# A graph layer's row gather: one of 32 indirect gathers done as 128 one-row DMAs by byte offset, and all block transfers issued by ScalarE

## The chip, the cores and the metric

The kernel runs on one core of a Trainium2 chip. The metric is the device time of one execution in microseconds (us). Five engines run their own instruction streams side by side: TensorE (PE; its weight loads are shown as PEld), VectorE (DVE), ScalarE (ACT), GpSimd (POOL) and SyncE (SP). They wait for one another through semaphores only. A "q" behind an engine's name (SPq, DVEq) marks its sequencer: register work, branches, loads of registers and the issuing of DMAs. The core has 16 DMA engines, which carry the transfers that SP, ACT and POOL issue.

## The reference, cut to what matters

```python
def _gcn_layer(x, W, b, edge_weight, edge_src, edge_dst):
    support = x @ W
    msgs = support[edge_src] * edge_weight[:, None]
    agg = jax.ops.segment_sum(msgs, edge_dst, num_segments=N_NODES)
    return agg + b
# x: 12500 x 256 float32; 200000 edges, sorted by dst; dst = 12500 * u**2, src uniform
x = x + gnn(layernorm(x))      # two layers: elu(_gcn_layer(..., W1, b1)), elu(_gcn_layer(..., W2, b2))
x = x + ffn(layernorm(x))      # ffn: H = gelu(x @ W1 + b1), 256 -> 1024; softmax gate over 8 experts;
                               # the chosen expert's H @ Wd[e] + bd[e], times its probability
```

## The kernel before

**Stages.** From 0 to about 115 us the kernel normalises the rows of x into a table in HBM (`xn_scratch`), loads the edge lists and turns them into tables in SBUF. Then come two graph layers, of about 1,960 and 2,010 us. The second one also runs the dense part of the feed-forward on each block of 128 nodes as soon as the layer has finished it. From about 4,125 us on the nodes are sorted by expert and the experts' products run.

**A graph layer.** The edges are cut into 392 groups of 512, four tiles of 128 edges each. Eight groups are an iteration (`ITERS` = 49), four are a half. POOL (line 537) gathers for each tile 128 rows of 1 KB by indirect DMA: 32 gathers in an iteration, into a ring `rows` of 8 slots by 4 tiles. Before slot 0 and slot 4 it waits for `s_idx`, the indices that DVE stages (line 778) for half h+2 only after it has added the four groups of half h; before each slot it waits for `s_mm`, the products of the group that held the slot. DVE (line 847) builds for each group a matrix S of weights (128 edges by 96 nodes per tile). PE (line 1164) multiplies the rows by S, 8 products in a group; each ran as two MATMUL and two LDWEIGHTS. DVE (line 886) adds the result to `aggT` at the group's first node, and builds the S of the group after next (line 888). PE uses two buffers of S, so the third group after any point needs DVE's add of the first.

**Ticks.** After each half comes, by a table of numbers, a tick for one block of nodes (98 blocks, 98 halves). In layer 1 ACT copies the block out of `aggT` (line 625), PE multiplies it by the layer's weights (1174), DVE adds the bias (895), ACT and DVE form the elu, and SP stores the result to `h_scratch` (437). In layer 2 the tick also holds the feed-forward's steps for older blocks: PE lines 1186 to 1212, DVE 924 to 955, ACT 653 to 664, and on SP the load of x's block (452) and the stores of x1 (462) and of the hidden rows (467). DVE and ACT wait for those stores by `s_free` and `s_payfree`, which SP raises.

**Loops.** Each engine has its own hardware loop over the 49 iterations, with both halves written out. PE and DVE hold each half twice: with code for groups that reach past the 96 nodes of S, and without (lines 1237 and 973 choose). The loops turn at line 1233 (PE), 969 (DVE), 669 (ACT) and 529 (POOL); SP has one loop over the blocks in each layer (435, 473).

## Time and profile before

| | us |
|---|---|
| median of 3 runs | 4690.26 |
| lowest of the runs | 4685.44 |
| the profiled execution, its span | 4687.7 |
| POOL busy | 3267.9 (70%) |
| PE busy | 3478.1 (74%) |
| DVE busy | 1979.0 (42%) |
| ACT busy | 1116.6 (24%) |

The profile is of one execution. Its span runs from the first instruction to the last. Issuing a DMA, register work and branches are not counted as busy, so SP has no busy time, and POOL's busy time lacks the 0.3 us between two gathers. "Idle before it" in a row is the time that the engine stood still ahead of the instruction, with what ended it; "issue" there is time for which the profile shows no releaser.

### The profile page before, as it was taken

The page shows a single profiled execution, that of the slowest core. Times are in us where ns is not written, and L with a number is a line of the kernel's source. Part 1 is how long each engine was busy: PE and PEld are TensorE (multiplying, and loading weights), DVE is VectorE, ACT ScalarE, POOL GpSimd, SP SyncE. Part 2 cuts the span into 40 slices and gives each one's busy share as a digit, 9 for nine tenths or more (in the row PEclk, how much of TensorE's full clock was granted, in tenths as well). Part 3 has the DMA queues.
Part 4 walks back from the last instruction along what each step waited for, and adds up shares of the span by engine and source line. Part 5 has one row for each costly group of instructions (what it writes and reads, how often), then busy time and mean ns, then how long its engine had stood idle before and what let it go on. Part 6 is the DMA issues. An engine that isn't in the chain of part 4 may idle for free.

```text
span 4687.7 us, 84720 instructions
## 1 busy us (share of the span) xinstructions
PE 3478.1 (74%) x21458; PEld 3215.9 (69%) x21459; DVE 1979.0 (42%) x6592; ACT 1116.6 (24%) x1692; POOL 3267.9 (70%) x3405
## 2 busy tenths in 40 slices
PE   2766676676666666667877777777777777859999
PEld 1666666665666665657777777777777777748887
DVE  8333333333333333334454454445444444573333
ACT  4111111111111111113333333333333333311111
POOL 5777777777777777767777777777777777524444
PEclk7766666667666666669999999999999999889999
DMA  8333333333333333334444444444444444335554
GB/s 278 113 113 112 113 111 112 113 112 112 113 111 113 112 113 112 113 95 128 145 139 144 144 137 143 145 144 139 141 145 139 142 143 145 116 127 169 180 175 150
DMA packets 266657, 627.24 MB, mean 134 GB/s; under 512 B 63397, under 2 KB 135034, under 8 KB 265922
## 3 DMA queue, kind: packets, MB, share of 16 engines
q0 software_dynamic: 170688, 492.87, 36.6%
q1 hardware_dynamic: 95362, 129.30, 7.9%
q14 instruction: 595, 4.87, 0.3%
q8 instruction: 12, 0.20, 0.0%
HBM read 519.25 MB, written 103.63 MB: 133 GB/s over the span
## 4 chain that ended last, share of the span: by engine, by line
PE 40%; issue 21%; POOL 15%; DVE 11%; DVEq 5%; DMA 5%; ACT 2%; POOLq 0%; ACTq 0%; SPq 0%
PE pA L1164 23%; POOL rows L537 15%; PE pA L1286 8%; PE pB L1202 4%; DMA rows<-xn_scratch,idx 3%; DVE S L847 2%; PE pZ L1174 1%; ACT L653 1%; DVE work L929 1%; DVEq L359 1%; PE pC L1276 1%; PE pB L1276 1%; DVE work L924 1%; DVEq L876 1%; DVE aggT L886 1%
## 5 line engine op out<-in xcount | busy, mean ns | idle before, releaser
L1164 PE MATMUL pA<-S,rows 128*128 128x96 f32 x12544 | 2040.8, 337 | 716.0 <-DVE S L847 314.5
L1164 PEld LDWEIGHTS pA<-S,rows 128*128 128x128 f32 x12544 | 1966.6, 249 | 834.3 <-issue 421.7
L537 POOL DMA_INDIRECT rows<-h_scratch,idx x1568 | 1502.3, 958 | 516.5 <-issue 492.5
L537 POOL DMA_INDIRECT rows<-xn_scratch,idx x1568 | 1490.2, 950 | 485.2 <-issue 458.1
L886 DVE TENSOR_TENSOR aggT<-aggT,pA 128x192 f32 x784 | 277.3, 354 | 2061.0 <-PE pA L1164 1421.4
L625 ACT ACT_TABLE_LOAD x196 | 251.5, 1283 | 3002.5 <-DVE aggT L886 3000.4
L847 DVE TENSOR_SCALAR S<-iota_w,tdst,twgt 128x96 f32<-128x96 f32 x3152 | 843.9, 343 | 5.5 <-issue 2.6
L1174 PE MATMUL pZ<-wg,stage 128*128 128x256 f32 x784 | 295.2, 514 | 252.6 <-ACT stage L625 252.6
L1202 PE MATMUL pB<-work,w 128*128 128x128 f32 x3232 | 389.2, 279 | 33.2 <-DVE work L929 33.2
L1202 PEld LDWEIGHTS pB<-work,w 128*128 128x128 f32 x3232 | 370.1, 192 | 42.0 <-DVE work L929 42.0
L1286 PE MATMUL pA<-aggT,work 128*128 x1680 | 381.7, 380 | 0.0
L1174 PEld LDWEIGHTS pZ<-wg,stage 128*128 128x128 f32 x784 | 176.6, 250 | 296.8 <-ACT stage L625 275.6
L1286 PEld LDWEIGHTS pA<-aggT,work 128*128 128x128 f32 x1680 | 311.7, 191 | 39.5 <-issue 0.9
L562 POOL DMA_INDIRECT out_dram<-aggT,ids x105 | 107.2, 1021 | 226.6 <-DVE ids L1087 180.1
L1186 PE MATMUL pC<-identg,work 128*128 128x136 f32 x1236 | 164.5, 283 | 3.4 <-ACT work L664 1.8
L1105 DVE TENSOR_TENSOR aggT<-pA,aggT 128x256 f32<-128x256 f32 x105 | 44.6, 425 | 277.3 <-PE pA L1286 277.3
L1186 PEld LDWEIGHTS pC<-identg,work 128*128 128x128 f32 x1236 | 151.9, 192 | 4.0 <-issue 2.0
L557 POOL DMA_INDIRECT aggT<-pay_scratch,ids x105 | 101.6, 967 | 40.8 <-issue 34.0
L664 ACT ACT_TABLE_LOAD x100 | 128.3, 1283 | 1.8
L653 ACT ACT_TABLE_LOAD x100 | 128.3, 1283 | 1.7
L929 DVE TENSOR_TENSOR work<-pB,b1col 128x1024 f32<-128x1024 f32 x102 | 123.9, 1214 | 3.1 <-PE pB L1202 2.4
L901 DVE TENSOR_SCALAR zexp<-zexp 128x256 f32<-128x256 f32 x198 | 62.4, 315 | 134.2 <-ACT zexp L634 134.2
(175 smaller groups left out, 2107.9 us busy)
## 6 DMA issues: line engine op xcount, KB each, us to landing
pay_scratch<-work SPq DMA_DIRECT2D x98, 512.0 KB
rows<-xn_scratch,idx POOLq DMA_INDIRECT x1568, 2.8
rows<-h_scratch,idx POOLq DMA_INDIRECT x1568
h_scratch<-work SPq DMA_DIRECT2D x98, 128.0 KB
pay_scratch<-work SPq DMA_DIRECT2D x98, 128.0 KB, 2.5
work<-in_x_dram SPq DMA_DIRECT2D x97, 128.0 KB
rows<-in_x_dram SPq DMA_DIRECT2D x24, 512.0 KB, 5.2
xn_scratch<-rows SPq DMA_DIRECT2D x24, 512.0 KB, 5.9
```

Of the source, the lines that this page charges most:

```text
L537: pool.indirect_dma_start(rows[:, s, t, :], None, source, bass.IndirectOffsetOnAxis(at, 0))\
L625: act.activation(stage[:, :, :], aggT[:, :, block_of(j)], ACT.Copy).then_inc(s_stage[layer], 1)
L653: act.activation(bstd[:, 0:1], bmv[:, 1:2], ACT.Sqrt, bias=epsc[:, :]).then_inc(s_std2, 1)
L664: act.activation(HT, hid, ACT.Gelu).then_inc(s_gelu, 1)
L847: last = v.tensor_scalar(S[:, half, t, :], iota_w[:, :], tdst[:, t, bass.ds(g, 1)], twgt[:, t, bass.ds(g, 1)], ALU.is_equal, ALU.mult)
L886: v.tensor_tensor(to, to, pA[:, u % 2, 0:KC * W].rearrange("p (k n) -> p k n", k=KC), ALU.add)\
L929: v.tensor_tensor(hid, pB[:, :].rearrange("p (k n) -> p k n", k=KH), b1col[:, :].unsqueeze(2).to_broadcast([P, KH, P]), ALU.add).then_inc( ...
L1164: last = mm(to[:, k * W:(k + 1) * W], rows[:, slot, t, k * P:(k + 1) * P], Sx[:, t, :], start=(t == 0), stop=(t == T - 1))
L1174: last = mm(pZ[:, 0:C], stage[:, k, :], wg[:, k, :], start=(k == 0), stop=(k == KC - 1))
L1186: mm(pF[:, m // PERB, m % PERB, :], HT[:, m, :], identg[:, m, :], start=True, stop=True)
L1202: last = mm(pB[:, m * P:(m + 1) * P], w1[:, k, m * P:(m + 1) * P], xnT[:, k, :], start=(k == 0), stop=(k == KC - 1))
L1286: last = mm(pA[:, q % 2, 0:C], HTx[:, q % 2, m, :], wdk[:, m, bass.ds(ec, C)], start=(m == 0), stop=(m == KH - 1))
```

## The change

**Rows.** The last tile (t = 3) of the last slot (slot 7) in each iteration is no longer gathered by POOL. Its 128 rows come by 128 plain DMAs of one row each, 88 from SP and 40 from ACT, with the row's byte offset (index times 1024) in a register. POOL has 31 gathers in an iteration. The rows of even iterations go to `rows[:, 7, 3]`, those of odd ones to a new tile `xrow`. SP starts an iteration's batch once the first group of the iteration before is multiplied, ACT does its 40 in two lots of 20, ahead of the two ticks of the iteration before. Both wait, before a batch, for all their earlier rows.

**Offsets.** DVE shifts the last tile's indices to bytes; ACT stores them to HBM (`row_offsets`) in the first stage. SP and ACT load the next 88 and 40 offsets by a DMA of their own, and read them into registers with a TENSOR_LOAD of up to 32 registers each.

**Loops.** Because of the two buffers, PE, ACT and SP now loop over pairs of iterations (24 turns and one iteration written out behind them). DVE's and POOL's loops stay.

**Block transfers.** ACT issues all of them, at the end of its tick: the store to `h_scratch`, and in layer 2 the hidden rows, x1 and the next x block. SP's loops over blocks and `s_free`, `s_payfree` are gone; waits go to the stores' own semaphores. So that no block needs a special case, x is first copied, HBM to HBM, into `x_padded` (12.8 MB, by SP after the weights), and ACT waits for that copy before its first layer.

**Small.** `tsrc` is int16; `iota_w` and `tnum` are parts of `iota_p`.

```diff
+        def pairs(eng, body):
+            with eng.Fori(0, ITERS // 2) as q:
+                for par in range(2):
+                    body(2 * q + par, par)
+            body(ITERS - 1, (ITERS - 1) % 2)
...
+        def load_offsets(eng, layer, who, i):
+            n, lane = (XSP, XACT)[who], (0, XSP)[who]
+            row = i * -SLOTS + (XPAD + NG - SLOTS)
+            eng.dma_start(xoff[who][:, :], xoff_d[bass.ds(row, 1), lane:lane + n]).then_inc(s_ring[layer][who], 16)
+
+        def single_rows(eng, layer, who, i, par, first, last):
+            n, lane = (XSP, XACT)[who], (0, XSP)[who]
+            source = (xn_d, h1_d)[layer].rearrange("n c -> (n c)").bitcast(u8)
+            to = row_buffer(par).bitcast(u8)
+            for at in range(first, last, XREGS):
+                upto = min(at + XREGS, last)
+                if at == 0:
+                    hold(eng, s_mm[layer], SLOTS * i + 1)
+                    hold(eng, s_ring[layer][who], 16 * (i + 1))
+                _, values = nc.values_load_multi_w_load_instructions(
+                    xoff[who][0:1, at:upto], engines=[eng.engine], min_val=0, max_val=(N - 1) * ROWB,
+                    skip_runtime_bounds_check_because="a src is a node's number")
+                if at == 0:
+                    hold(eng, s_xrow[layer][who], 16 * (i * n + 1))
+                if upto == n:
+                    load_offsets(eng, layer, who, i + 1)
+                for k, v in enumerate(values, lane + at):
+                    eng.dma_start(to[k:k + 1, :], source[bass.ds(v, ROWB)].rearrange("(a n) -> a n", a=1))\
+                       .then_inc(s_xrow[layer][who], 16)
...
 SP
-            with sp.Fori(0, NB) as b:
-                sp.wait_ge(s_elu[0], b + 3)
-                sp.dma_start(h1_d[block_of(b), :], hout).then_inc(s_h1st, 16)
-                sp.wait_ge(s_h1st, 16 * (b + 1))
-                sp.sem_inc(s_free[0], 1)
...
+            sp.dma_start(xp_d[0:N, :], x[:, :]).then_inc(s_xpad, 16)
+            sp.dma_start(xp_d[N:NPAD, :], x[0:NPAD - N, :]).then_inc(s_xpad, 16)
+            sp.wait_ge(s_xoffst, 3 * 16)
+            for layer in range(2):
+                start_rows(sp, layer, 0)
+                pairs(sp, lambda i, par: single_rows(sp, layer, 0, i, par, 0, XSP))
+                sp.wait_ge(s_ring[layer][0], 16 * (ITERS + 1))
...
 POOL
-                        for t in range(T):
+                        for t in range(XT if s == SLOTS - 1 else T):
...
 ACT, layer 1's tick and layer 2's
+                act.wait_ge(s_elu[0], j + 2)
+                act.dma_start(h1_d[block_of(j - 1), :], hout).then_inc(s_h1st, 16)
...
-                act.wait_ge(s_payfree, j + 1)
+                act.wait_ge(s_payst, 16 * (j + 1))
...
+                act.wait_ge(s_payc, j + 2)
+                act.dma_start(pay_d[block_of(j - DEPTH), 0:HID], payh).then_inc(s_payst, 16)
+                if flows(1, j):
+                    act.wait_ge(s_elu[1], j + 2)
+                    act.dma_start(pay_d[block_of(j - 1), HID:PAY], x1).then_inc(s_x1st, 16)
+                if flows(0, j):
+                    act.dma_start(xb, xp_d[block_of(j), :]).then_inc(s_xb, 16)
...
+            def iteration(layer, i, par):
+                for half in range(2):
+                    if not isinstance(i, int):
+                        single_rows(act, layer, 1, i + 1, 1 - par, half * XACT // 2, (half + 1) * XACT // 2)
+                    h = 2 * i + half
+                    _, start, end = half_flags(act, h)
+                    ticks(act, start, end, lambda j: (tick1, tick2)[layer](j, h))
+
+            act.wait_ge(s_xoffst, 3 * 16)
+            act.wait_ge(s_xpad, 2 * 16)
             for layer in range(2):
+                start_rows(act, layer, 1)
+                single_rows(act, layer, 1, 0, 0, 0, XACT)
+                pairs(act, lambda i, par: iteration(layer, i, par))
...
 PE
             for layer in range(2):
-                with pe.Fori(0, ITERS) as i:
-                    for half in range(2):
...
+                pairs(pe, lambda i, par: iteration(layer, i, par))
```

**SP, the loop of layer 1.** Before, one turn of the loop stores one block; the rows are the whole loop (a DMA's row names where it writes and what it reads).

```order
L435 UNCONDITIONAL_BRANCH
L435 ISA
L437 ISA
L437 DMA h_scratch<-work 128x256
L438 ISA
L435 REGISTER_ALU
L435 COMPARE_AND_BRANCH
```

Now one iteration's part of the loop reads as follows (`xoff_sp` holds the 88 offsets); the loop holds it twice, the second time with `xrow` for `rows`.

```order
L334 ISA
L420 TENSOR_LOAD xoff_sp
L334 ISA
L428 DMA rows<-xn_scratch 1x1024 x32
L420 TENSOR_LOAD xoff_sp
L428 DMA rows<-xn_scratch 1x1024 x32
L420 TENSOR_LOAD xoff_sp
L408 ISA
L408 DMA xoff_sp<-row_offsets 1x88
L428 DMA rows<-xn_scratch 1x1024 x24
```

SP went from one store per tick to 89 DMAs and three loads of registers per iteration.

**ACT, between two ticks of layer 2.** Before, the GELU of one tick (L664) is followed by the loop's own rows and the next half's flags (L359).

```order
L664 ACT_TABLE_LOAD
L664 ACTIVATE work<-work 128x1024
L370 REGISTER_ALU
L370 COMPARE_AND_BRANCH
L369 UNCONDITIONAL_BRANCH
L359 ISA
L359 TENSOR_LOAD regs
```

Now, from the tick's last transfer (L699) to the next half's flags (L370):

```order
L699 DMA work<-x_padded 128x256
L381 REGISTER_ALU
L381 COMPARE_AND_BRANCH
L380 UNCONDITIONAL_BRANCH
L420 TENSOR_LOAD xoff_act
L408 ISA
L408 DMA xoff_act<-row_offsets 1x40
L428 DMA xrow<-h_scratch 1x1024 x20
L370 ISA
L370 TENSOR_LOAD regs
```

Three transfers at the tick's end and 20 rows with their register load now stand between one tick of ACT and the next.

## Rows read from the trace of the kernel before

**Rows 1.** The page's first line.
```profile
span 4687.7 us, 84720 instructions
```
**Rows 2.** Windows of equal stages: window, length, PE, PEld, DVE, ACT, POOL busy (count), clock, DMA share, GB/s.
```profile
0.00:120.00 120.00, 28.66 (x140) 25.17 (x141) 95.87 (x342) 48.85 (x89) 60.97 (x69) 0.72 0.88 274
230.00:1200.00 970.00, 667.51 (x3282) 604.89 (x3281) 312.85 (x1157) 130.91 (x240) 734.76 (x773) 0.65 0.39 112
2260.00:3200.00 940.00, 737.24 (x5507) 701.47 (x5506) 462.52 (x1564) 336.29 (x460) 705.82 (x737) 0.92 0.48 142
```
**Rows 3.** Line 537, all instructions: duration ns min/median/max, first and last start.
```profile
L537 POOL DMA_INDIRECT rows<-xn_scratch,idx x1568: 942/946/1256, 89.9 to 2056.4; - x196
```
**Rows 4.** Timeline of layer 1, POOL and PE: start, busy, [idle before, releaser].
```profile
1007.04 0.95 POOL L537 DMA_INDIRECT rows<-xn_scratch,idx  x1 [0.30 <-issue]
...
1011.27 3.70 PE L1164 MATMUL pA<-S,rows 128*128 128x96 f32 x16 [0.90 <-DMA rows<-xn_scratch,idx]
```
**Rows 5.** Waits in layer 1, window 100:2040: total us, times, longest.
```profile
PE pA L1164 <- DMA rows<-xn_scratch,idx: 227.3, 124, 3.1
```
**Rows 6.** Waits in layer 2, window 2260:4070: total us, times, longest.
```profile
PE pA L1164 <- DVE S L847: 169.7, 45, 4.3
POOL rows L537 <- DVE idx L778: 23.1, 37, 1.0
```
**Rows 7.** Timeline of PE over one iteration of layer 2, from tick to tick.
```profile
3018.79 7.51 PE L1164 MATMUL pA<-S,rows 128*128 128x96 f32 x64 [1.04 <-issue]
...
3034.34 0.38 PE L1212 MATMUL pT<-ident,work 128*128 128x128 f32 x2
3036.29 3.78 PE L1164 MATMUL pA<-S,rows 128*128 128x96 f32 x32 [1.57 <-issue]
3043.84 6.55 PE L1164 MATMUL pA<-S,rows 128*128 128x96 f32 x32 [3.76 <-DVE S L847]
...
3059.71 0.54 PE L1164 MATMUL pA<-S,rows 128*128 128x96 f32 x3 [0.90 <-issue]
```
**Rows 8.** Sequencers at the loops' turns in that iteration (lines 969, 876, 1233; start last).
```profile
L969 DVEq COMPARE_BRANCH  x1: 72/72/72, 3034.2 to 3034.2; - x1
L969 DVEq FUSED_REGOPS  x1: 93/93/93, 3037.6 to 3037.6; - x1
L973 DVEq COMPARE_BRANCH  x1: 72/72/72, 3038.7 to 3038.7; - x1
L876 DVEq FUSED_REGOPS  x3: 71/190/190, 3041.3 to 3045.0; - x3
L1233 PEldq FUSED_REGOPS  x1: 74/74/74, 3034.7 to 3034.7; - x1
```
**Rows 9.** SP's queue: one-row DMAs and their neighbours, and a DMA with its address in a register.
```profile
3.15 0.23 SPq L394 DMA_DIRECT2D aggT<-in_dst_dram  x1
3.42 0.40 SPq L390 DMA_DIRECT2D aggT<-in_src_dram  x1
L437 SPq MOVE h_scratch<-work x98: 29/29/29, 144.2 to 2071.6; - x98
```
**Rows 10.** Line 359, a load of one register on ACT's sequencer, and SP's store landing.
```profile
L359 ACTq TENSOR_LOAD <-regs x196: 264/268/462, 113.5 to 4056.4; - x196
DMA to landing us min/median/max: 1.7/2.5/3.2
```
**Rows 11.** Timeline of ACT in layer 2, first and last of a tick and the next.
```profile
3010.15 1.28 ACT L625 ACT_TABLE_LOAD   x1 [16.77 <-DVE aggT L886]
...
3016.50 1.06 ACT L664 ACTIVATE work<-work 128x1024 f32<-128x1024 f32 x1
3027.13 1.28 ACT L625 ACT_TABLE_LOAD   x1 [9.57 <-DVE aggT L886]
```
**Rows 12.** Timeline around the start of layer 1: SP's last load, ACT's first tick.
```profile
92.47 0.53 SPq L429 DMA_DIRECT2D b1col<-in_L_ffn_b_dram  x1
126.69 1.28 ACT L625 ACT_TABLE_LOAD   x1 [33.97 <-DVE aggT L886]
```

More of the change, by code:

```diff
@@ L85, in bass_gnn_then_routed_ffn @@
     KWIN = (N - 1) // W
+    XT = T - 1
+    XSP, XACT, XREGS = 88, 40, 32
+    XPAD = 2 * SLOTS
+    ROWB = 4 * C
     LNC = NB // T
@@ L269, in bass_gnn_then_routed_ffn @@
         s_elu = [sem(f"elu_ready_{l}") for l in range(2)]
-        s_free = [sem(f"elu_store_done_{l}") for l in range(2)]
         s_eln = [sem(f"elu_step_{l}") for l in range(2)]
@@ L372, in ticks, with source_stored, row_buffer, start_rows @@
                                             "the table's last end is the number of blocks"))
+        def pairs(eng, body):
[3 more added lines that the diff above has]
+            body(ITERS - 1, (ITERS - 1) % 2)
+        def source_stored(eng, layer):
+            if layer == 0:
+                eng.wait_ge(s_xst[0], 16 * (LNI + 2))
+                for s in range(1, SLOTS):
+                    eng.wait_ge(s_xst[s], 16 * LNI)
+            else:
+                eng.wait_ge(s_h1st, 16 * (NB + 2))
+        def row_buffer(par):
+            return xrow[:, :] if par else rows[:, SLOTS - 1, XT, :]
+        def load_offsets(eng, layer, who, i):
[21 more added lines that the diff above has]
+                       .then_inc(s_xrow[layer][who], 16)
+        def start_rows(eng, layer, who):
+            eng.sem_inc(s_xrow[layer][who], 16)
+            load_offsets(eng, layer, who, 0)
+            source_stored(eng, layer)
         @block.sync
@@ L521, in _ @@
             for layer, source in ((0, xn_d), (1, h1_d)):
-                if layer == 0:
-                    pool.wait_ge(s_xst[0], 16 * (LNI + 2))
-                    for s in range(1, SLOTS):
-                        pool.wait_ge(s_xst[s], 16 * LNI)
-                else:
-                    pool.wait_ge(s_h1st, 16 * NB)
+                source_stored(pool, layer)
                 with pool.Fori(0, ITERS) as i:
@@ L1158, in _, with products @@
             pe.sem_inc(s_y, 2)
-            def products(slot, Sx, to, semaphore):
+            def products(slot, par, Sx, to, semaphore):
                 for k in range(KC):
                     for t in range(T):
-                        last = mm(to[:, k * W:(k + 1) * W], rows[:, slot, t, k * P:(k + 1) * P], Sx[:, t, :],
+                        edge = row_buffer(par) if slot == SLOTS - 1 and t == XT else rows[:, slot, t, :]
+                        last = mm(to[:, k * W:(k + 1) * W], edge[:, k * P:(k + 1) * P], Sx[:, t, :],
                                   start=(t == 0), stop=(t == T - 1))
@@ L1225, in edges_half, with iteration @@
                                 pe.wait_ge(s_ovS[layer], w + 1)
-                                products(s, Sov, pOV, s_ovmm[layer])
+                                products(s, par, Sov, pOV, s_ovmm[layer])
                     pe.wait_ge(s_S[layer], g + 1)
                     pe.wait_ge(s_add[layer], g + 1)
-                    products(s, S[:, s % 2, :, :], pA[:, s % 2, :], s_mm[layer])
+                    products(s, par, S[:, s % 2, :, :], pA[:, s % 2, :], s_mm[layer])
             pe.wait_ge(s_w, 8 * 16)
-            for layer in range(2):
-                with pe.Fori(0, ITERS) as i:
-                    for half in range(2):
-                        h = 2 * i + half
-                        ovf, start, end = half_flags(pe, h)
-                        with pe.If(ovf > 0):
-                            edges_half(layer, i, h, half, True)
-                        with pe.Else():
-                            edges_half(layer, i, h, half, False)
-                        ticks(pe, start, end, (tick1, tick2)[layer])
+            def iteration(layer, i, par):
+                for half in range(2):
+                    h = 2 * i + half
+                    ovf, start, end = half_flags(pe, h)
+                    with pe.If(ovf > 0):
+                        edges_half(layer, i, par, h, half, True)
+                    with pe.Else():
+                        edges_half(layer, i, par, h, half, False)
+                    ticks(pe, start, end, (tick1, tick2)[layer])
+            for layer in range(2):
+                pairs(pe, lambda i, par: iteration(layer, i, par))
             for j in range(NB, NB + DEPTH):
```

102 lines of the change are left out of this document (48 added, 54 removed).

## The prediction

> **What bounds the kernel now.** I read the windows of equal stages first. In layer 1 POOL issues 773 gathers in 970 us, one in 1.255 us; in layer 2 it issues 737 in 940 us, one in 1.275 us [rows 2]. A gather is 0.95 us of work and 0.30 us of gap [rows 3, 4]. So an iteration of 32 gathers takes 40.2 us in layer 1 and 40.8 in layer 2, and at first sight POOL bounds both layers.
>
> The waits tell the layers apart. In layer 1 PE waits for the gathered rows, 124 times for 227 us [rows 4, 5]. There POOL is the bound. In layer 2 no wait of PE's products for gathered rows stands in the list: what they wait for is S from DVE, and it is POOL that waits, for the indices that DVE stages after finishing a half, 37 times, up to 1.0 us each [rows 6]. The timeline of one iteration says what PE does instead. It runs slots 4 to 7 at once (7.51 us), a tick until 3034.72, slots 0 and 1 from 3036.29, stands 3.76 us, slots 2 and 3 until 3050.39, the next tick, and is back at slot 4 at 3059.71 [rows 7]. From 3018.79 to 3059.71 is 40.9 us, the same 40.8 as above, and none of it is a wait for gathers. So PE's chain sets layer 2's period, and POOL, ready some 8 groups ahead, only fills it.
>
> The 3.76 us come from DVE. At its loop's turn the branch is at 3034.2 and the next instruction at 3037.6, 3.3 us later; the branch that skips the overflow code is at 3038.7, the next instruction at 3041.3, 2.5 us later. PE turns its loop in the same place within 0.2 us [rows 8]. I read this as DVE fetching code that a jump left behind, and PE finding its own at hand.
>
> **The sum.** It is made against this execution's span of 4687.7 us [rows 1]; the median of the runs, 4690.26, is 2.6 us above it, and is used as span plus 2.6.
>
> Layer 1, one gather less. 49 x 1.25 us = **-61 us**, if nothing else becomes the bound. SP must deliver its 88 rows within 31 x 1.25 = 38.8 us. The nearest row is the one-row load of line 394: 0.23 us of issue, and 0.27 us from start to the next start; with its address in a register a DMA has a MOVE of 0.03 us ahead of it, about 0.07 us with its gap [rows 9]. I take 0.355 us a row, between 0.34 and 0.37: 88 rows are 31.2 us. The offsets' own DMA is 0.45 us, the holds some 0.35 us, and the wait for the earlier rows to land, after the last issue, about 2 (a store lands in 1.7 to 3.2 us [rows 10]), under which the first register load can hide. That is 34 us plus two register loads. A load of one register takes 0.27 us [rows 10]; a load of 32 is not in the trace. Its bounds are 0.27 us and 32 x 0.27 = 8.6 us. It is one instruction, so I take 0.3 to 1.5 us, near the lower end: SP needs 35 to 37 us and is in time. The point from which it is not is (38.8 - 34) / 2 = 2.4 us a load. ACT's 40 rows are 14.2 us in a period in which it works some 7 in layer 1: hidden.
>
> The start of layer 1. ACT now waits for the 12.8 MB copy, which SP issues behind its last load at 93.0 [rows 12]. The first stage moved 274 GB/s with the DMA engines 88% busy [rows 2], so the copy takes at least 12.8 MB / 311 GB/s = 41 us, and at most 95 if gathers take their 112 GB/s beside it and reads and writes of HBM hinder each other. I take 47 (the 274): the copy ends at 140. Then ACT loads offsets (2.5), issues 40 and 20 rows (21.3) and comes to its first tick at about 165; before it did so at 126.69 [rows 12]. POOL starts at 89.9 [rows 3] and can run to the end of half 2, 12 groups or 59 us, so to 149; for half 3 it needs DVE through half 1, which is ACT's tick (5 us) and four groups (9 us) later: 179. **+30 us**, with 24 to 78 as bounds.
>
> Layer 2, one gather less: **0**. PE's chain does not wait for POOL; POOL's shorter iteration turns into longer waits for indices.
>
> Layer 2, PE's longer loop. The loop now holds two iterations. From the order of instructions, with each product as four (front: 8 products are 16 MATMUL and 16 LDWEIGHTS), PE's body in layer 2 grows from about 1,170 instructions to about 2,350, in layer 1 from 950 to 1,900. The trace shows a body of some 500 on DVE that stalls at each turn and one of 1,170 on PE that does not. Whether 2,350 does is open: below, nothing; above, DVE's 3.3 us at each turn and 2.5 us at each of four jumps over overflow code [rows 8], 13.3 us a turn. I think the turn and the first jump miss (5.8 us), and that 3.75 of it hides behind the wait for DVE at the same place [rows 7], leaving 2.1; for the three later jumps I take a third of 2.6, 0.9 each, since DVE's own code has mostly arrived by its second jump. 4.8 us x 24 turns = **+115 us**, bounds 0 and 230. In layer 1 PE has waits for gathers to use up, and I cost it at nothing.
>
> The Trainium skill (Runtime: NRT & Kernel Launch, Instruction fetch mechanics) says that PE's instruction memory holds 2,048 instructions and the other engines' 512, and that a taken branch outside the window waits for a fetch. By it layer 2's body is too long and layer 1's just fits, which is the term above; the trace agrees as far as its two bodies go.
>
> ACT in layer 2. In the shorter gap it starts ticks at 3010.15 and 3027.13, 17.0 us apart, and works until 3017.56 [rows 11]. It now adds three transfers (1.35 us), the offsets' DMA (0.45), 20 rows (7.1), a register load (0.3 to 1.5) and flags (0.9): 7.4 + 10.1 + 0.3 to 1.5 = 17.8 to 19.0. It is late by 0.8 to 2 us in one tick of two, but PE's own stalls stretch the same gap. I take 0.2 us x 49 = **+10**, bounds 0 and 100. DVE's waits on the stores are the old ones; the x block is asked for some 3 us later than before and has half a period to land.
>
> The tail: SP no longer sits behind the last stores and loads the experts' weights some 25 us earlier, into the last ticks' stores: **+2**. The small edits: 0, DVE's extra work lies in the first stage beside the x loads.
>
> Sum: -61 + 30 + 0 + 115 + 10 + 2 = +96; 4687.7 + 96 + 2.6 = 4786 us.
>
> **The rivals.**
> *No stall on PE.* The longer body finds its code as now. For it: PE shows no gap at any turn [rows 8]. Then -61 + 30 + 10 + 2 = -19: about 4670.
>
> *SP becomes the bound.* If a load of 32 registers takes 4.3 us (half of the upper bound), SP needs 34 + 9 + 2 = 45 us per iteration in both layers: +5 x 49 + 4 x 49 over today, +30: about 5160, and 5,700 at the upper bound. It decides from 2.4 us a load. For it: the one-register load is almost all round trip. Against: one instruction, one address. The Trainium skill (same page and section) gives some 200 ns per register even in bulk; by that a load of 32 would be 6.4 us, SP would need about 50 us, and the time be near 5,500. No run yet shows it.
>
> *Every jump misses.* 230 us instead of 115: about 4900.
>
> *Both layers shorten.* If in layer 2 it is POOL after all that paces PE, through the indices, then 2 x 61 less, with a start-up of 30: about 4600. Against it: PE's waits have no gathers in layer 2 [rows 6].
>
> **How the numbers follow.** Forecast 0.38 (own range 4730 to 4850); no stall 0.22; SP the bound 0.18; every jump 0.12; both shorten 0.10. The predicted time is the first's, 4786. The range leaves out the last and most of SP's: 4640 to 5150. Faster by over 2% (below 4596, about what this measurement can tell from no change) needs both layers: 0.08. Within 2% (to 4784) are the no-stall case, half of the forecast's own spread, and the rest of the last: 0.42. Slower 0.50.
>
> **What would show it.** Gathers per us on POOL: one in 1.25 with 31 an iteration in layer 1, 38.8 us; 40.8 or more in layer 2, with longer waits for indices. A gap on PE's sequencer between the loop's branch and the next instruction, 2 to 3.5 us, in layer 2 only. SP's register loads: their duration decides the third case at once. ACT's first tick of layer 1 near 165. I am wrong about layer 2 if its iterations get shorter than 40.8, and about SP if its rows stand back to back with PE waiting for them in slot 7.

## The result and the profile after

The changed kernel takes 5097.44 us (median of 4 runs, 5094.62 to 5102.15), against 4687.85 us before: a ratio of 1.0876, 95% interval 1.0859 to 1.0894. The forecast was 4786. Some of the experiments' kernels first ran while the kernel before itself took 6591 to 6918 us; their times are not compared with those of the table below, and all but one of them ran again beside a kernel before of some 4685 us (labels with b or c).

The windows and the gathers' line show where the 407 us between the two spans lie. First the page's first line, then windows as in [rows 2] with the start of layer 1 ahead of them, and that start in the kernel before; then POOL's gathers as in [rows 3] (line 555 is the old 537).

```profile
span 5094.6 us, 111092 instructions
```
```profile
90.00:230.00 140.00, 43.89 (x224) 39.95 (x225) 44.74 (x119) 15.78 (x21) 67.77 (x72) 0.57 0.58 178
230.00:1200.00 970.00, 595.76 (x3445) 542.55 (x3445) 333.30 (x1213) 136.37 (x250) 733.61 (x770) 0.70 0.41 118
2260.00:3200.00 940.00, 661.00 (x4560) 630.57 (x4560) 378.83 (x1291) 277.00 (x381) 561.88 (x588) 0.84 0.40 120
```
```profile
90.00:230.00 140.00, 84.55 (x456) 77.62 (x456) 65.25 (x201) 21.81 (x36) 106.28 (x111) 0.67 0.44 119
```
```profile
L555 POOL DMA_INDIRECT rows<-xn_scratch,idx x1519: 940/946/1204, 91.8 to 2050.6; - x190
L555 POOL DMA_INDIRECT rows<-h_scratch,idx x1519: 940/946/1191, 2068.1 to 4465.7; - x190
```

Layer 1: 770 gathers in 970 us against 773, so 31 take 39.05 us and 32 took 40.16. That is 54 us in 49 iterations, but layer 2 starts only 7.7 us earlier (2068.1, before 2075.8): the start of layer 1 gave back 46. Layer 2: 588 gathers in 940 us, 49.6 us an iteration against 40.8; from first to last gather 2397.6 us against 1999.4, **+398**. Behind the last gather the kernel runs for another 628.9 us against 612.5, +16. Together -8 + 398 + 16 = +406.

What PE does in layer 2, as in [rows 7], from two windows of its timeline:

```profile
3031.07 10.32 PE L1218 MATMUL pA<-S,rows 128*128 128x96 f32 x64 [5.19 <-issue]
...
3050.27 0.41 PE L1266 MATMUL pT<-ident,work 128*128 128x128 f32 x2 [0.68 <-ACT work L687]
3054.15 8.21 PE L1218 MATMUL pA<-S,rows 128*128 128x96 f32 x54 [3.47 <-issue]
...
3073.13 0.38 PE L1266 MATMUL pT<-ident,work 128*128 128x128 f32 x2
3080.42 9.58 PE L1218 MATMUL pA<-S,rows 128*128 128x96 f32 x64 [6.91 <-issue]
```

Two things are new. PE stands 5.2 and 6.9 us ahead of halves, with no releaser. And 3.5 us are lost ahead of a half in which nothing of PE's is slow (3054.15). A half has 32 products, each two MATMULs with a weight load ahead of each: 64 parts. The 64 parts behind a long stand take 9.6 to 10.3 us. That alone is not new: in [rows 7] one half of an iteration took 7.51 us, and the other 3.78 + 6.55 = 10.3 around the 3.76 us for which PE waited for S. The long stands are explained by PE's own branches. A turn of the doubled loop has four halves: here the third begins at 3031.07, the fourth at 3054.15 (10 of its parts stand in rows of their own), the next turn's first at 3080.42. The first three rows are the turn (line 388), the branch over the overflow code (1296) in the first half behind it, and the same in the third half; the fourth row has all turns between 2200 and 4450 us. Below them is the old loop's turn, over both layers.

```profile
L388 PEldq COMPARE_BRANCH  x1: 5247/5247/5247, 3071.4 to 3071.4; - x1
L1296 PEldq COMPARE_BRANCH  x1: 2344/2344/2344, 3077.6 to 3077.6; - x1
L1296 PEldq COMPARE_BRANCH  x1: 4173/4173/4173, 3026.5 to 3026.5; - x1
L388 PEldq COMPARE_BRANCH  x22: 4397/4827/5367, 2281.4 to 4353.8; - x22
```
```profile
L1233 PEldq COMPARE_BRANCH  x98: 73/216/223, 145.9 to 4095.5; - x98
```

On PE the stall is the branch's own duration; on DVE it was a gap behind a short branch [rows 8]. With the other two branches over overflow code (0.36 and 0.44) it is some 12 us in two iterations. The page's list of DMA queues shows the same as traffic, first after, then before. Queue q8 is the one that carries PE's code: e1 below, which changes nothing but PE's loops, has 489 packets on it and q14 as before.

```profile
q8 instruction: 489, 8.01, 0.7%
q14 instruction: 956, 7.83, 0.5%
```
```profile
q14 instruction: 595, 4.87, 0.3%
q8 instruction: 12, 0.20, 0.0%
```

8.01 MB in 489 packets is 16.4 KB each, about ten at each of 48 turns; before, PE's queue carried 12 packets in all. The Trainium skill (Runtime: NRT & Kernel Launch, Instruction fetch mechanics) has code come in blocks of 16 KiB, 256 instructions; the packets' size agrees.

### The profile page after: what moved, and what is told of

Same layout as the page of the kernel before. It is cut to its first block, busy times and chain, and to the rows that moved or that the text cites. A ratio compares the mean times of both kernels' runs of the same rounds, so it can differ in the third digit from the quotient of the medians.

```text
span 5094.6 us, 111092 instructions
## 1 busy us (share of the span) xinstructions
PE 3427.8 (67%) x21458; PEld 3181.0 (62%) x21459; DVE 1980.3 (39%) x6594; ACT 1116.8 (22%) x1692; POOL 3172.0 (62%) x3305
## 3 DMA queue, kind: packets, MB, share of 16 engines
q8 instruction: 489, 8.01, 0.7%
## 4 chain that ended last, share of the span: by engine, by line
PE 38%; issue 28%; ACTq 17%; DVE 8%; ACT 3%; DMA 3%; DVEq 2%; POOL 1%; SPq 0%; POOLq 0%
PE pA L1218 22%; ACTq L428 12%; PE pA L1348 7%; PE pZ L1228 4%; PE pB L1256 4%; ACTq L420 3%; ACTq L370 1%; DVE S L900 1%; ACT stage L651 1%; DVE work L982 1%; DMA x_padded<-in_x_dram 1%; PE pC L1338 1%; PE pB L1338 1%; ACT L681 1%; DMA pay_scratch<-work 1%
## 5 line engine op out<-in xcount | busy, mean ns | idle before, releaser
L1218 PE MATMUL pA<-S,rows 128*128 128x96 f32 x12352 | 1952.1, 334 | 964.8 <-issue 867.2
L1218 PEld LDWEIGHTS pA<-S,rows 128*128 128x128 f32 x12352 | 1908.9, 248 | 1060.6 <-issue 998.5
L555 POOL DMA_INDIRECT rows<-h_scratch,idx x1519 | 1450.7, 955 | 964.4 <-DVE idx L830 510.1
L555 POOL DMA_INDIRECT rows<-xn_scratch,idx x1519 | 1446.3, 952 | 521.2 <-issue 455.1
L900 DVE TENSOR_SCALAR S<-iota_p,tdst,twgt 128x96 f32<-128x96 f32 x3152 | 836.9, 340 | 10.1 <-issue 10.1
```

Of the source, the lines that this page charges most:

```text
L555: pool.indirect_dma_start(rows[:, s, t, :], None, source, bass.IndirectOffsetOnAxis(at, 0))\
L900: last = v.tensor_scalar(S[:, half, t, :], iota_w[:, :], tdst[:, t, bass.ds(g, 1)], twgt[:, t, bass.ds(g, 1)], ALU.is_equal, ALU.mult)
L1218: last = mm(to[:, k * W:(k + 1) * W], edge[:, k * P:(k + 1) * P], Sx[:, t, :], start=(t == 0), stop=(t == T - 1))
```

## Experiments

For each kernel: layer 1 and layer 2 from first to last gather, the time behind the last gather, the median, and the ratio to the kernel before that ran beside it. The bodies of PE's loop are given as counts of instructions; these are estimates from the order of instructions, as in the prediction.

| kernel | layer 1 | layer 2 | behind | median us | ratio (95%) |
|---|---|---|---|---|---|
| before | 1966.5 | 1999.4 | 612.5 | 4688 | |
| after | 1958.8 | 2397.6 | 628.9 | 5097 | 1.088 (1.086 to 1.089) |
| e1, PE's pairs alone | 1969.3 | 2076.2 | 611.5 | 4766 | 1.017 (1.015 to 1.019) |
| e10b, the same, code shifted | 1973.2 | 2151.9 | 614.9 | 4840 | 1.033 (1.032 to 1.035) |
| e2, after, PE's loop short | 1959.1 | 2006.6 | 620.0 | 4697 | 1.002 (1.001 to 1.003) |
| e3, after, ACT without rows | 1945.3 | 2201.3 | 625.5 | 4882 | 1.042 (1.040 to 1.044) |
| e4, both | 1943.0 | 1999.7 | 626.7 | 4678 | 0.998 (0.997 to 0.999) |
| e5b, after, ACT's hold earlier | 1959.0 | 2221.6 | 625.9 | 4918 | 1.049 (1.047 to 1.051) |
| e6b, after, copy waited later | 1951.7 | 2393.7 | 630.0 | 5083 | 1.084 (1.083 to 1.086) |
| e8b, rows in layer 1 only | 1949.4 | 2005.0 | 623.1 | 4690 | 1.001 (1.000 to 1.002) |
| e9, that without the copy | 1924.0 | 1998.0 | 611.5 | 4651 | 0.993 (0.991 to 0.994) |
| p1c, before, 385 dead instructions | 1969.7 | 2552.6 | 625.5 | 5259 | 1.123 (1.121 to 1.125) |

**PE's code against ACT's rows (e1 to e4).** The theory of PE's code: its long branches make layer 2. The rival: ACT's rows do, and the branches lie in PE's waiting time. e1 is the kernel before with

```diff
-                with pe.Fori(0, ITERS) as i:
+                with pe.Fori(0, ITERS // 2) as q:
+                    for par in range(2):
+                        iteration(layer, 2 * q + par)
+                iteration(layer, ITERS - 1)
```

> The kernel before, and only PE's loops turn every two iterations (24 turns and one iteration written out); gathers, SP, ACT, DVE stay. Theory 1, PE's code: in the changed kernel PE's branch at the loop's turn takes up to 5.2 us in layer 2 and the branches over the overflow code 2.3 and 4.2 us, about 12 us in two iterations, and the products behind them run at the lower clock. Then the same branches take as long here, layer 2's iteration grows from 40.8 to 46 to 48 us, layer 1 stays at 40.2 (POOL paces it), and the time is 4940 to 5030. Theory 2, ACT: the 400 us of layer 2 come from ACT's rows, which hold up its ticks, and PE's long branches lie in time in which PE would wait for ACT anyway. Then this kernel is within 30 us of before, 4690 to 4720.

e2 is the changed kernel with

```diff
-                        edge = row_buffer(par) if slot == SLOTS - 1 and t == XT else rows[:, slot, t, :]
+                        edge = rows[:, slot, XT - 1, :] if slot == SLOTS - 1 and t == XT else rows[:, slot, t, :]
...
-                pairs(pe, lambda i, par: iteration(layer, i, par))
+                with pe.Fori(0, ITERS) as i:
+                    iteration(layer, i, 0)
```

> The changed kernel, but PE's loops turn every iteration, with one iteration's code, as before. So that this needs no second buffer in the code, PE's product for the last tile of slot 7 reads the tile beside it (rows[:, 7, 2]) and not the single rows; the single rows are still fetched and waited for. The output is not the reference's. Theory 1, PE's code: the long branches are gone, layer 2's iteration falls from 49.4 to 43 us or less (ACT's lateness of some 3 us in one half stays), time 4720 to 4800. Theory 2, ACT: layer 2 stays at 47 us or more, time above 4980.

So e2 multiplies tile 2 of slot 7 in place of tile 3, and its output is not the reference's. e3 drops ACT's `single_rows`, their offsets and PE's wait for them (88 of 128 rows are fetched, so its output is not the reference's either); e4 has both edits.

> The changed kernel without ACT's 40 rows and their offsets in either layer (128 fetched rows become 88; xrow is cleared once by POOL; the output is not the reference's). ACT still issues all block transfers. Theory 1, PE's code: the long branches stay, and only what ACT's lateness costs goes: layer 2's iteration 46 to 48 us, time 4930 to 5030. Theory 2, ACT: layer 2's iteration back to 41 us, time 4680 to 4710.

> Both edits together: PE's one-iteration loops (last tile of slot 7 read from rows[:, 7, 2]) and no rows from ACT; output not the reference's. Both theories: layer 2's iteration is back at 40.8 us or a little under, layer 1 stays at 39.2 us, and the time is 4650 to 4690. If it is above 4720, a third cause is at work (SP's row transfers beside the gathers, or ACT's block transfers).

Measured: 4766, 4697, 4882 and 4678. e1 lies between the theories, e2 better than the first one had it, e3 below it, e4 as expected. The four corners show how much belongs to each part and how much only to both together:

| layer 2, us | ACT without rows | ACT with rows |
|---|---|---|
| PE's loop short | 1999.7 | 2006.6 |
| PE's loop long | 2201.3 | 2397.6 |

PE's code costs 202 us without ACT's rows; ACT's rows cost 7 us without PE's long code; another 189 come only where both are. SP's rows and ACT's block transfers are both in e4 and cost layer 2 nothing. Two questions followed: why PE's code costs 77 alone and 202 in this company, and how ACT's rows come to cost 196.

**The place of the code (e10b).** e1 with 14 instructions more ahead of layer 2's loop, 6 that run and 8 that never do:

```diff
+                if layer == 1:
+                    _, never, _ = half_flags(pe, 0)
+                    with pe.If(never > 200):
+                        for _ in range(2):
+                            mm(pOV[:, 0:W], rows[:, 0, 0, 0:P], Sov[:, 0, :], start=True, stop=True)
```

> As e1 (the kernel before, PE's loops in pairs), with 14 more instructions of PE's ahead of layer 2's loop, 8 of them never run: the loop's code stands 14 instructions later, where it stands in the changed kernel. PE's edit cost 77 us alone (e1) and 204 beside the single rows and ACT's transfers (e3 against e4). Theory 1, the place of the code decides where PE runs out of it: a pause of 2 to 3 us moves into a group, once in two iterations, with the lower clock behind it, layer 2 grows by 60 to 120 us, time 4825 to 4885. Theory 2, the other transfers (SP's rows, ACT's stores) take PE's slack away or make the fetch slower: as e1, 4760 to 4775.

Measured 4840: the first theory. PE's timeline where the pause stands, e1, then e10b:

```profile
3056.61 2.00 PE L1164 MATMUL pA<-S,rows 128*128 128x96 f32 x16 [1.09 <-issue]
3060.18 5.60 PE L1164 MATMUL pA<-S,rows 128*128 128x96 f32 x48 [1.57 <-DVE aggT L886]
```
```profile
3009.22 1.21 PE L1164 MATMUL pA<-S,rows 128*128 128x96 f32 x9 [1.09 <-issue]
3012.19 8.05 PE L1164 MATMUL pA<-S,rows 128*128 128x96 f32 x55 [1.76 <-issue]
```

A part is two instructions, a weight load and a matmul. 14 instructions of shift moved the pause from behind the 16th part to behind the 9th: 7 parts, 14 instructions. It stands there in all 22 pairs of iterations that were read in each trace (behind the 10th part in e3, behind the 7th in e5b and the changed kernel). So PE pauses at a fixed place of the code, which I read as running out of it; the releaser named in e1's row is by the way. In e1 the 48 parts behind it take 5.60 us at a granted clock of 1.00; in e10b the 55 behind it take 8.05 at 0.79. The changed kernel:

```profile
3004.95 1.78 PE L1218 MATMUL pA<-S,rows 128*128 128x96 f32 x7 [3.53 <-issue]
...
3008.80 8.67 PE L1218 MATMUL pA<-S,rows 128*128 128x96 f32 x57 [2.08 <-issue]
```

Over all of layer 2 it reads as follows. Each number is the stand ahead of a half plus its 64 parts, pauses and waits for S included, in us: the mean of the 22 pairs. The doubled loop turns ahead of half 1; the kernel before turns ahead of halves 1 and 3.

| | half 1 | half 2 | half 3 | half 4 | clock in half 2 |
|---|---|---|---|---|---|
| before | 15.5 | 8.5 | 15.6 | 8.5 | 1.00 |
| e1 | 18.2 | 10.1 | 13.6 | 8.5 | 0.99 |
| e10b | 18.1 | 13.1 | 14.4 | 8.5 | 0.77 |
| e3 | 18.0 | 13.9 | 15.0 | 9.4 | 0.73 |
| e5b (below) | 18.5 | 14.3 | 15.4 | 9.6 | 0.75 |
| after | 18.1 | 16.2 | 15.5 | 13.1 | 0.66 |

e1 and e10b differ by 3.0 us in half 2, the one with the pause, where the clock falls, and by 0.8 in half 3. These make the 76 us between their layers 2, of the 125 that separate e1's from e3's. The other 49 are spread over halves 2 to 4 and were not separated: they come with the other parts of the change.

**ACT's hold (e5b).** In the changed kernel ACT stands after its tick until PE has multiplied the first group of the next iteration. Its rows are not late because they are long, but because they begin late:

```profile
3024.71 0.69 ACTq L699 DMA_DIRECT2D work<-x_padded  x1
...
3035.00 0.35 DVE L939 TENSOR_TENSOR aggT<-aggT,pA 128x192 f32 x1 [9.92 <-PE pA L1218]
...
3036.57 7.00 ACTq L428 DMA_DIRECT2D rows<-h_scratch  x20
...
3041.59 0.36 DVE L939 TENSOR_TENSOR aggT<-aggT,pA 128x192 f32 x1 [0.46 <-PE pA L1218]
```
```profile
3045.08 1.28 ACT L651 ACT_TABLE_LOAD   x1 [19.36 <-DMA rows<-h_scratch]
```

From 3025.7 to 3034.8 ACT does nothing; PE's group ends at 3034.8, ACT loads registers and issues 20 rows, and comes to its tick at 3045.08, 3.1 us after the half's last add (3041.59 + 0.36). In layer 2's waits that is a row that e3 and e5b don't have (window 2260:4400):

```profile
DVE zexp L954 <- ACT zexp L660: 116.1, 42, 4.0
```

DVE's tick is late by almost as much, and PE's next half waits for the tick's last result. Most of the 3.47 us ahead of 3054.15 is that; with the earlier hold (e5b) 1.53 are left at the same place. The edit:

```diff
-                    hold(eng, s_mm[layer], SLOTS * i + 1)
+                    hold(eng, s_mm[layer], SLOTS * i + (1 if who == 0 or isinstance(i, int) else 0))
```

> The changed kernel with one number changed: inside the loops ACT starts its rows when the iteration's last group before has been multiplied, and not one group later (the tile that the rows go to is free by then). Output is the reference's. Theory 1, the hold: ACT's 20 rows cost 215 us (5097 against 4882) because PE, late from its long branch, releases them only with its first group, and ACT then comes to its tick some 3 us after the half is added. With the earlier release ACT issues them while PE stands: 4885 to 4930. Theory 2, the length of ACT's work (20 rows, register load, offsets and turn, some 11 us in each half) is what costs: 5040 or more.

Measured 4918: the first theory. 176 of the 196 us go with one count of one semaphore. By the table above 1.9 us go in half 2 and 3.5 in half 4, where the clock rises from 0.77 to 0.97; the rest lies in the ticks. ACT's rows of the same place now begin while PE stands in its long branch (3048.3 to 3054.0), and the tick follows the add:

```profile
3050.06 7.06 ACTq L428 DMA_DIRECT2D rows<-h_scratch  x20
3065.10 1.28 ACT L651 ACT_TABLE_LOAD   x1 [16.95 <-DVE aggT L939]
```

**How long PE's loop may be (p0b, p1c).** The kernel before, with products behind a condition that is never true at the end of layer 2's loop: 12 groups' worth (385 instructions), or 6 (190).

```diff
+                        with pe.If(start > 200):
+                            for _ in range(12):
+                                products(0, Sov, pOV, s_ovmm[1])
```

> The kernel before with some 385 instructions never run at the end of PE's loop in layer 2 (body about 1,560 in place of 1,170). In p1b, against a kernel before of 6905 us, the loop's turn took 5.8 us, the branch over the padding 3.8 and every second branch over the overflow code some 3.7. Theory 1: such branches cost time as in e1, where 256 us of them in layer 2 made 77: with some 500 us of them here, 4850 or more. Theory 2, nearly all of it hides in PE's waits: 4690 to 4740.

> The kernel before with some 190 instructions never run at the end of PE's loop in layer 2: a body of about 1,365 instead of 1,170. In p0 (ratio 1.000, against a kernel before of 6905 us) no branch of the loop was longer than 0.3 us. Theory 1, the body still fits: branches of 0.22 us, time 4680 to 4700. Theory 2, the length of the body costs something by itself, in proportion: half of what p1c showed, 4900 or more.

p1c measured 5259, +576 us, for code that never runs: the first theory. Its turn (line 1233), the branch over the dead code (1243), and below them the turn in p0, the first run of p0b's kernel:

```profile
L1233 PEldq COMPARE_BRANCH  x45: 4617/5112/6152, 2246.2 to 4564.7; - x45
L1243 PEldq COMPARE_BRANCH  x45: 3739/4494/5044, 2241.8 to 4560.0; - x45
```
```profile
L1233 PEldq COMPARE_BRANCH  x98: 73/216/237, 177.0 to 6313.5; - x98
```

With a body of about 1,365 instructions no branch of layer 2's iterations is longer than 0.5 us, in p0 and in p0b (ratios 1.000 and 0.9985; the kernel before took 6905 and 6918 us beside them, so the forecast times could not be tested and no price is read from them, only the branches). With about 1,560 every turn is slow. For this loop the limit lies between. It is not a matter of doubling the loop.

**The start of layer 1 (e6b, e8b, e9).** e6b moves ACT's wait for the copy to layer 2.

> The changed kernel, but ACT waits for the copy of x into x_padded only before layer 2, where it first reads it. Output is the reference's. Theory 1: the wait for the copy is what delays layer 1's first tick (from 126.7 to about 180 us) and costs 30 to 40 us: 5057 to 5067. Theory 2, the copy's traffic beside the gathers and ACT's 60 rows cost it (as in e8b, where 33 gathers fewer were issued by 230 us although nobody waited for the copy): 5085 or more.

Measured 5083, -14 us: two us short of the second theory's bound, and 16 above the first one's range. The first tick moved from 179.8 to 164.5, and layer 1 gained 7 us by it. e8b has single rows in layer 1 alone; it also has e5b's hold and e6b's later wait.

> Single rows in layer 1 only; in layer 2 POOL gathers all 32, and PE and ACT loop over single iterations; the copy is waited for before layer 2; ACT's hold is the earlier one; ACT issues all block transfers. Output is the reference's. Theory 1: layer 1 keeps its gain of 1 us in an iteration (39.2 against 40.2) and layer 2 is as before: 4640 to 4665. Theory 2: block transfers on ACT or the copy cost something of their own in the unchanged layer 2: 4690 or more.

Measured 4690, at the second theory's bound and 25 us above the first one's range; but layer 2 is only 6 us longer than before, and its own trace shows the rest at the start. PE waits 21 us for a group's gathers, in just the time in which the copy runs (50.3 us from issue to landing; 48.6 in the changed kernel):

```profile
93.33 3.23 SPq L494 DMA_DIRECT2D x_padded<-in_x_dram  x1
...
140.51 3.70 PE L1221 MATMUL pA<-S,rows 128*128 128x96 f32 x16 [21.08 <-DMA rows<-xn_scratch,idx]
```

From 90 to 230 us POOL issues 78 gathers, 72 in the changed kernel, and 111 in the kernel before (both in the section on the result). e9 takes the copy away: in layer 2 SP does the block transfers as before.

> As e8b (single rows in layer 1 only, 4689 us there), and without the copy of x: in layer 2 SP loads x's blocks and stores the hidden rows and x1 as in the kernel before, ACT issues only layer 1's stores. Output is the reference's. In e8b PE waited 21 us for the second group's gathers while the copy ran, POOL issued 78 gathers from 90 to 230 us where the kernel before issued 111, and layer 2 and the tail took 6 and 10 us more than before. Theory 1, the copy's traffic holds up the start: layer 1 runs at 38.9 us an iteration from the start, about 1915 to 1930 us, the rest is as before: 4630 to 4655. Theory 2, ACT's 60 rows ahead of the first tick and the rows themselves cost the start: 4665 to 4690.

```profile
90.00:230.00 140.00, 64.21 (x349) 57.81 (x350) 57.17 (x167) 20.34 (x31) 93.43 (x97) 0.62 0.41 113
```
```profile
L588 POOL DMA_INDIRECT rows<-xn_scratch,idx x1519: 940/946/1471, 91.5 to 2015.5; - x190
```

Measured 4651, the first theory; ratio 0.993 (0.991 to 0.994): of the versions with the reference's output the only one that beats the kernel before, by less than 1%. 97 gathers by 230 us, layer 1 42.5 us shorter. At the kernel before's pace 1519 gathers take 1906 us; against that the changed kernel loses 53, e6b 46, e8b 43 and e9 18. So the wait for the copy is worth some 7 us, the copy's own traffic 25 to 28, and 18 are left. As much later e9's first tick comes (144.9 against 126.69), ACT's first 60 rows standing ahead of it.

**The first runs of these kernels.** Their expectations, mostly in the words of the repeats':

> The changed kernel with one number changed: inside the loops ACT starts its rows when the iteration's last group before has been multiplied, and not one group later (the tile that the rows go to is free by then). Output is the reference's. Theory 1, the hold: ACT's 20 rows cost 215 us (5097 against 4882) because PE, late from its long branch, releases them only with its first group, and ACT then comes to its tick some 3 us after the half is added. With the earlier release ACT issues them while PE stands: 4885 to 4930. Theory 2, the length of ACT's work (20 rows, register load, offsets and turn, some 11 us in each half) is what costs: 5040 or more.

> The changed kernel, but ACT waits for the copy of x into x_padded only before layer 2, where it first reads it. Output is the reference's. Theory 1: the wait for the copy is what delays layer 1's first tick (from 126.7 to about 180 us) and costs 30 to 40 us: 5057 to 5067, first tick near 150 (ACT's own 60 rows still stand ahead of it). Theory 2: the copy's traffic beside the gathers and ACT's rows cost it: 5085 or more.

> Single rows in layer 1 only; in layer 2 POOL gathers all 32 and PE and ACT loop over single iterations; the copy is waited for before layer 2; ACT's hold is the earlier one; ACT issues all block transfers. Output is the reference's. Theory 1: layer 1 keeps its gain of 1 us in an iteration (39.2 against 40.2) and layer 2 is as before: 4640 to 4665. Theory 2: block transfers on ACT or the copy cost something of their own in the unchanged layer 2: 4690 or more.

> The kernel before, with some 390 instructions of code that is never run (12 groups' products behind a condition that is never true) at the end of PE's loop in layer 2: the body grows from about 1,170 to 1,560 instructions, of which 1,170 run. If the body's length decides from about 1,900 on, no branch of PE's is longer than 0.5 us and the time is 4680 to 4700. If it decides earlier, the loop's turn takes 3 to 5 us; most of it lies in the 3.8 us for which PE waits for S there, and the time is 4690 to 4740.

> As e1 (the kernel before, PE's loops in pairs), with 14 more instructions of PE's ahead of layer 2's loop, 8 of them never run: the loop's code stands 14 instructions later, where it stands in the changed kernel. PE's edit cost 77 us alone (e1) and 204 beside the single rows and ACT's transfers (e3 against e4). In the traces the one difference inside PE's products is a pause in the middle of a group, once in two iterations (24 in layer 2, 2.3 us each, in e3 and the changed kernel, with the lower clock behind it; in e1 PE stands 1.6 us between two groups and keeps its clock). Theory 1, the place of the code decides where PE runs out of it: the pause moves into a group here too, layer 2 grows by 60 to 120 us, time 4825 to 4885. Theory 2, the other transfers (SP's rows, ACT's stores) make the fetch slower or take PE's slack away: as e1, 4760 to 4775.

> As p1: the kernel before with some 385 instructions never run at the end of PE's loop in layer 2 (body about 1,560 in place of 1,170). In p1, against a kernel before of 6591 us, the loop's turn took 5.9 us and the branch over the padding 3.7 us. The same branches are as long here; about 3.8 us of each turn hide in the wait for S. Theory 1: 9 to 11 us of branches a turn, 4 to 7 of them on the path, in 49 turns: 4880 to 5030. Theory 2, nearly all of it hides: 4690 to 4740.

> The same with some 190 instructions never run: body about 1,365. If the limit lies between 1,365 and 1,560, no branch of PE's in layer 2 is longer than 0.5 us, and the time is 4685 to 4700. If 1,365 is already past it, the turn takes 3 to 6 us.

e5 took 7186 us, e6 7116 and e8 7233 beside a kernel before of 6591 (ratios 1.089, 1.080, 1.098), p1 6763 in its one run; e10 6937, p1b 7035 and p0 6903 beside 6905 (1.006, 1.019, 1.000), p0b 6905 beside 6918. The same edits rank otherwise there than in the table, so those times decide nothing here. What is used from them is how long PE's branches are: 5.8 us at p1's and p1b's turn, 0.22 at p0's and p0b's (medians).

## Why the prediction was wrong, step by step

**Layer 1, one gather less:** -61 forecast, -54 measured; no run explains the 7 between. SP was in time, by little: its rows come every 0.345 us (32 in 11.05), but a load of 32 registers takes 2.04 us where I took 0.3 to 1.5, and the case turned at 2.4. (The rival's upper bound was added up wrongly: two loads of 8.6 us give SP 53 us and a time near 5,960, not 5,700.)

```profile
L420 SPq TENSOR_LOAD <-xoff_sp x294: 1673/2038/3297, 142.0 to 4441.6; - x147
```
```profile
PE pA L1218 <- DMA xrow<-xn_scratch: 2.3, 1, 2.3
```

The second row is all that PE waited for single rows between 300 and 2000 us. 2.04 us for 32 registers is 64 ns each; the rule of some 200 ns per register (Trainium skill, Runtime: NRT & Kernel Launch, Instruction fetch mechanics) does not hold here.

**The start:** +30 forecast, +46 measured. The copy ended about where I had it (94.7 + 48.6 = 143, forecast 140), the first tick came at 179.8 and not at 165. The step that failed is that POOL "can run to the end of half 2". It stopped one half earlier, at 130.7, because PE had no rows to multiply while the copy ran, and so finished half 0 at 153.5 and not at 125.9:

```profile
136.41 3.70 PE L1218 MATMUL pA<-S,rows 128*128 128x96 f32 x16 [15.20 <-DMA rows<-xn_scratch,idx]
146.83 6.72 PE L1218 MATMUL pA<-S,rows 128*128 128x96 f32 x32 [6.72 <-DMA rows<-xn_scratch,idx]
```

I priced the wait for the copy and not its traffic, which is three to four times as much. That the sum came within 16 us is luck: the wait, which made all of my 30, is worth 7.

**Layer 2, one gather less:** 0, right. e4, with all that remains, has 1999.7 us against 1999.4.

**PE's longer loop:** +115 forecast. The mechanism was right: slow branches in the long body, in layer 1 hidden (e1's layer 1 is 2.8 us longer, though the same loop's turn takes some 3.7 us in the changed kernel's), in layer 2 not. Alone it is 77 (e1), below my term, since more of it hides than the 3.75 us that I took: the wait for S goes in both iterations of a pair, and half 3 is even shorter than before. e1's waits of layer 2 have 11 us left of the 170 for S [rows 6]. With the code near its place in the changed kernel it is 152 (e10b, whose pause is two parts from the changed kernel's), beside the other parts 202 (e3 less e4). What the term lacked is a pause in the middle of straight code, whose place 14 instructions decide, and the lower clock behind it: half 2 takes 13.1 us in place of 8.5. The parts behind the turn are no slower than before; there PE had lost its clock behind the wait for S already. Branch for branch I had 5.8 us for the turn and the first jump and 0.9 for each later one, 8.5 in all; measured are 7.6 for the first two, 4.2 for the third half's and 0.4 for the others, 12 in all.

**ACT in layer 2:** +10 forecast, +196 measured beside PE's long loop; this is the step that failed most: 186 of the 311 us by which the forecast was short. The length of ACT's work was right (with the loop short it costs 7; that its terms add to 9.8 and not to 10.1 changes nothing), and the sentence that "PE's own stalls stretch the same gap" was wrong. By the change ACT waits until the first group is multiplied (the `hold` on `s_mm`), and I never asked what that wait does when PE is the one that is late: PE's stall doesn't make room for ACT's rows, it moves their release. From the release to the half's last add PE and DVE need 6.8 us (3034.8 to 3041.6); ACT needs 10.3 to its tick.

**The tail:** +2 forecast, +16 measured. 4 of the 16 are layer 2's own slowness: from the last gather to the end of the last block's multiplication by the layer's weights it takes 24.6 us against 20.6 (31.5 in p1c, where nothing of the tail was changed). Behind that point it is 604.3 against 591.9, +12. Here the mechanism was named (the experts' weights come earlier, into the last stores), its size was not: the 8 MB are asked for at 4484.80, 35 us earlier against that multiplication and not 25, and ACT then waits for its hidden-row stores,

```profile
4484.80 22.88 SPq L504 DMA_DIRECT2D aggT<-in_L_ffn_Wd_dram  x8
```
```profile
ACT work L685 <- DMA pay_scratch<-work: 14.8, 4, 7.6
```

where the kernel before had no such wait. In e9, with the old order of SP's loads and stores, the tail is back at 611.5. That the weights and not the stores' new place on ACT lengthen those waits was not tested.

**The whole:** 4687.7 - 8 + 398 + 16 = 5094. Of layer 2's 398, 152 are PE's longer code near its place, 176 ACT's hold, 20 the rest of ACT's rows, and 49 are PE's code beside the other parts, left open. Against the forecast 186 us are missing in ACT's term, 87 in PE's (202 for 115), 16 at the start, 14 in the tail and 7 in layer 1's gather. The hold's 176 and the rest's 20 exist only beside PE's long code. The measured time lies inside the outer range of 4640 to 5150, but that range reached so high for SP as the bound, which did not come; that it holds is luck. Of the rivals, "no stall on PE", SP as the bound and the shorter layer 2 fell; "every jump misses" was nearest for PE (230 for 202), and none of them had ACT in it.

## What to carry to other kernels

Before a loop is unrolled for a second buffer, count the body, with the code in it that is jumped over: past a limit (here between some 1,365 and 1,560 instructions on PE) every turn pays, and dead code counts like live code. When an engine gets work behind a wait, ask who raises the semaphore, and what happens when that engine is late; a wait set one count too strict cost more here (176 us) than the long loop near its place (152), though only beside it. A copy with nobody waiting for it is still paid by the transfers beside it, so do without it (e9), or try to put it where the DMA engines are idle (not tried here).

## What the runs showed of the hardware

- PE's slow branch: 4.4 to 5.4 us at the turn of a body of about 2,350 instructions, 4.6 to 6.2 with about 1,560, 0.22 (median) with about 1,170 and 1,365. By the Trainium skill (Runtime: NRT & Kernel Launch, Instruction fetch mechanics: 2,048 instructions for PE) 1,560 would fit, and so would layer 1's 1,900, whose turn takes 3.7 us in its median. The measurement decides.
- PE's doubled loops fetched their whole code again at every turn, and some more. e8b, where only layer 1's loop is doubled, has 227 packets on PE's queue, 215 more than before; that is about 9 for each of 24 turns, for a body of about 1,900 instructions, 7.4 packets' worth at 256 in each. In layer 2 it is (489 - 227) / 24 = 11, for 9.2.
- A stand of 1.6 us between two groups left the granted clock at 1.00 (e1: 48 parts in 5.60 us behind it); one of 1.8 us inside a group was followed by 55 parts in 8.05 us at 0.79 (e10b). Whether the length or the place of the pause makes the difference was not tested.
- ACT and SP pause too where their doubled loops turn, as DVE did [rows 8]: in the changed kernel's layer 2 the first turn's branch is at 2281.6 on ACT and the next instruction at 2285.1, on SP 2231.0 and 2234.0. e2 has both loops and the same gaps (3.7 and 3.6 us in the median), and its layer 2 is 7 us longer than before. In e4, without its rows, ACT's loop turns in 0.2 us.
- One-row DMAs take 0.225 us of SP's queue and 0.235 of ACT's, some 0.33 to 0.35 from one to the next with their register's MOVE.
